# Attention's softmax on VectorE's 32x32 transposes in place of TensorE's

## The reference

```python
x = x + tanh(g_xattn) * attention(layernorm(x), ctx, ctx, mask, wq, wk, wv, wo)
#   q = rope(x @ wq), k = rope(ctx @ wk), v = ctx @ wv
#   softmax(q k^T / sqrt(128) + mask, over the 64 keys) @ v @ wo
x = x + tanh(g_ffn) * ffn(layernorm(x))
#   ((xf * in_scale) @ sign(W)^T) * out_scale + bias, scales from a softmax router
```

## Time and profile before

| | us |
|---|---|
| median of 3 runs | 1663.18 |
| span of the profiled execution (from the first to the last instruction; the page gives no other time of it) | 1658.5 |
| attention, first keys split to the last store of probabilities | 95.5 to 951.1 |
| projection, first to last w_lo | 957.0 to 1392.9 |

### The profile page before, as it was taken

How to read it: one execution, slowest core, us unless ns; L and a number is a source line. 1 busy time by engine, 2 the same in 40 slices (tenths; PEclk the granted TensorE clock), 3 DMA queues, 4 the chain that set the end, 5 groups by cost and what they waited for, 6 DMA issues and landing times. The chain is left out here.

```text
span 1658.5 us, 23370 instructions
## 1 busy us (share of the span) xinstructions
PE 1574.9 (95%) x7808; PEld 1299.9 (78%) x7808; DVE 965.7 (58%) x1670; ACT 664.2 (40%) x1271; POOL 673.3 (41%) x514
## 2 busy tenths in 40 slices
PE   6999999999999999999999689999999999389998
PEld 6878888888888888888888578888888888266776
DVE  6736666766667666666676545444444444646562
ACT  5812222322223222232222257666666665343342
POOL 6734443444434443444344234333333332323443
PEclk9999999999999999999999899999999999689999
DMA  7722212221222212222121595237923332723311
GB/s 273 255 76 64 64 45 64 70 74 39 71 63 70 63 38 71 75 64 54 52 63 38 190 366 173 77 99 269 335 77 101 101 101 78 247 76 140 119 65 58
DMA packets 90838, 183.27 MB, mean 111 GB/s; under 512 B 17152, under 2 KB 31872, under 8 KB 90752
## 3 DMA queue, kind: packets, MB, share of 16 engines
q1 hardware_dynamic: 84528, 169.94, 32.0%
q10 hardware_dynamic: 6256, 12.65, 2.1%
HBM read 129.07 MB, written 53.48 MB: 110 GB/s over the span
## 5 line engine op out<-in xcount | busy, mean ns | idle before, releaser
L46 PE MATMUL q_ps<-x_hi,w_hi 128*128 128x512 f32 x1024 | 405.1, 396 | 3.9 <-PEq L61 3.9
L48 PE MATMUL q_ps<-x_hi,w_lo 128*128 128x512 f32 x1024 | 402.2, 393 | 0.0
L47 PE MATMUL q_ps<-x_lo,w_hi 128*128 128x512 f32 x1024 | 401.3, 392 | 0.0
L869 DVE TENSOR_TENSOR vw_lo<-vw_ps,vw_hi 64x256 fp32r<-64x256 f32 x512 | 216.0, 422 | 237.5 <-ACT vw_hi L816 232.3
L594 POOL TENSOR_TENSOR q_lo<-rot,q_hi 128x512 fp32r<-128x512 f32 x128 | 191.8, 1518 | 268.4 <-ACT q_hi L563 268.4
L856 POOL TENSOR_TENSOR w_lo<-w_raw,w_hi 128x512 fp32r<-128x512 f32 x128 | 165.2, 1291 | 280.6 <-ACT w_hi L808 280.6
L816 ACT CAST vw_hi<-vw_ps 64x256 fp32r<-64x256 f32 x512 | 188.2, 368 | 142.0 <-PE vw_ps L48 130.5
L46 PEld LDWEIGHTS q_ps<-x_hi,w_hi 128*128 128x128 f32 x1024 | 192.9, 188 | 44.1 <-issue 4.1
L48 PEld LDWEIGHTS q_ps<-x_hi,w_lo 128*128 128x128 f32 x1024 | 192.6, 188 | 41.3
L47 PEld LDWEIGHTS q_ps<-x_lo,w_hi 128*128 128x128 f32 x1024 | 192.7, 188 | 40.5
L614 DVE TENSOR_TENSOR rot<-q_ps,cos_q 128x512 f32<-128x512 f32 x64 | 44.3, 692 | 288.0 <-PE q_ps L48 288.0
(11 more groups left out here) (130 smaller groups left out, 2566.4 us busy)
## 6 DMA issues: line engine op xcount, KB each, us to landing
w_raw<-in_wo SPq DMA_DIRECT2D x128, 256.0 KB, 2.6
w_raw<-in_wq SPq DMA_DIRECT2D x32, 512.0 KB, 5.2
probs_scratch<-pt_hi SPq DMA_DIRECT2D x64, 256.0 KB, 2.6
probs_scratch<-pt_lo SPq DMA_DIRECT2D x64, 256.0 KB, 3.2
x_hi<-probs_scratch SPq DMA_DIRECT2D x32, 512.0 KB, 5.9
x_lo<-probs_scratch SPq DMA_DIRECT2D x32, 512.0 KB, 7.8
x_in<-in_x SPq DMA_DIRECT2D x16, 512.0 KB, 4.1
attn_scratch<-ahead_y ACTq DMA_DIRECT2D x8, 1024.0 KB, 4.4
```

The source lines that it names most:

```text
L46: pe.matmul(out, hi, rhs_hi, start=first, stop=False, **kw)
L47: pe.matmul(out, hi, rhs_lo, start=False, stop=False, **kw)
L48: return pe.matmul(out, lo, rhs_hi, start=False, stop=last, **kw)
L869: done = nc.vector.tensor_tensor(vw_lo[at], vw_ps[i][b * SK:(b + 1) * SK, h, :], vw_hi[at].bitcast(F32), ALU.subtract)
```

## The change

The keys' heads are interleaved in blocks of 32 on the partitions of the scores: key half k, head h, 32 keys. VectorE adds the mask in the layout in which scores come (`masked`), transposes each 32x32 block of the [128, 512] tile in place of TensorE's turning, and reduces over 32 columns. A softmax row then lies in two partition halves, so the maximum and the sum are combined by a copy to PSUM and two operations of 64 partitions (`both_halves`). The product with the reciprocal is transposed again by VectorE (`pt`), ScalarE makes `pt_hi`, and GpSimd `pt_lo`, before that slot's product. The scores' copy by ScalarE and all eight turning matmuls go. The rotation keeps two products in PSUM (`rope_ps`). The stored probabilities have the interleaved order, and `load_probs` puts four blocks of 32 partitions back in the old one, one DMA each. Keys are loaded compactly and split in two halves of partitions; key_hi and key_lo are zeroed once in place of key_raw. The diff, cut:

```diff
 EARLY_P = 4
+BLK = 32
+NBLK = S // BLK
...
 def load_probs(sp, scratch, p_hi, p_lo, p_in, pair, hp):
 
     for n, part in enumerate((p_hi, p_lo)):
-        src = scratch["probs"][n, hp, :, pair * PB * S:(pair + 1) * PB * S]
-        sp.dma_start(part[:, hp].bitcast(F32), src).then_inc(p_in[hp], 16)
+        for k in range(2):
+            for h in range(2):
+                of, to = (2 * k + h) * BLK, (2 * h + k) * BLK
+                src = scratch["probs"][n, hp, of:of + BLK, pair * PB * S:(pair + 1) * PB * S]
+                sp.dma_start(part[to:to + BLK, hp].bitcast(F32), src).then_inc(p_in[hp], 16)
 
 
...
-        key_raw = sb("key_raw", [P, 2, B, P])
+        key_raw = sb("key_raw", [P, 2, B, SK])
         key_hi = sb("key_hi", [P, 2, B, P], F32R)
         key_lo = sb("key_lo", [P, 2, B, P], F32R)
         cos_q = sb("cos_q", [P, S])
         sin_q = sb("sin_q", [P, S])
-        mask = sb("mask", [P, B, TT, SK])
-        rot = sb("rot", [P, 4, S])
+        mask = sb("mask", [P, B, S])
+        prod = sb("prod", [P, 2, S])
+        rot = sb("rot", [P, 2, S])
         q_hi = sb("q_hi", [P, 2, S], F32R)
         q_lo = sb("q_lo", [P, 2, S], F32R)
-        scores_t = sb("scores_t", [P, S])
-        shifted = sb("shifted", [P, TT, 2, SK])
-        exps = sb("exps", [P, TT, 2, SK])
-        probs = sb("probs", [P, TT, 2, SK])
-        row_max = sb("row_max", [P, TT, 2])
-        row_sum = sb("row_sum", [P, TT, 2])
-        row_inv = sb("row_inv", [P, TT, 2])
+        masked = sb("masked", [P, S])
+        shifted = sb("shifted", [P, NBLK, BLK])
+        probs = sb("probs", [P, NBLK, BLK])
+        part_max = sb("part_max", [P, NBLK])
+        part_sum = sb("part_sum", [P, NBLK])
+        row_max = sb("row_max", [P, NBLK])
+        row_sum = sb("row_sum", [P, NBLK])
+        row_inv = sb("row_inv", [P, NBLK])
+        pt = sb("pt", [P, S])
         pt_hi = sb("pt_hi", [P, 2, S], F32R)
         pt_lo = sb("pt_lo", [P, 2, S], F32R)
         q_ps = [ps(f"q_ps{i}", [P, S]) for i in range(4)]
         st_ps = ps("st_ps", [P, S])
-        s_ps = ps("s_ps", [P, TT, 2, SK])
-        pt_ps = ps("pt_ps", [P, S])
+        s_ps = ps("s_ps", [P, NBLK, BLK])
+        rope_ps = ps("rope_ps", [P, S])
+        part_ps = ps("part_ps", [P, 2, NBLK])
...
         pt_lo_ready = sem("pt_lo_ready")
         pt_stored = following["pt_stored"]
 
         block = ctx.enter_context(nc.Block())
+
+        def own_block(part, h):
+
+            return part[h * HALF:(h + 1) * HALF].rearrange("f c b (k n l) -> f (c b) k n l", k=2, n=2)[:, :, :, h]
+
+        def raw_keys(h):
+
+            return key_raw[h * HALF:(h + 1) * HALF].rearrange("f c b (k l) -> f (c b) k l", k=2)
...
             def load_keys(g):
-                wait(sp, key_lo_ready, g)
+                wait(sp, key_lo_ready, 2 * g)
                 for c in range(2):
                     for h in range(2):
                         src = scratch["keys"][c].rearrange("(g f) t -> g f t", f=HALF)[bass.ds(g, 1)]
-                        sp.dma_start(key_raw[h * HALF:(h + 1) * HALF, c, :, h * SK:(h + 1) * SK],
+                        sp.dma_start(key_raw[h * HALF:(h + 1) * HALF, c],
                                      src.rearrange("o f (b s) -> (o f) b s", b=B)).then_inc(key_in, 16)
 
             def slot(g, j, last):
...
@@ -507,9 +521,9 @@
                 if has(g, j, 1):
                     b = (j - 1) % B
                     if j == 1:
-                        pe.wait_ge(key_hi_ready, g + 1)
-                        pe.wait_ge(key_lo_ready, g + 1)
-                    wait(pe, st_copied, u - 1)
+                        pe.wait_ge(key_hi_ready, 2 * (g + 1))
+                        pe.wait_ge(key_lo_ready, 2 * (g + 1))
+                    wait(pe, masked_ready, u - 1)
                     for c in range(2):
                         pe.wait_ge(q_hi_ready, 2 * u - 1 + c)
                         pe.wait_ge(q_lo_ready, 2 * u - 1 + c)
@@ -518,19 +532,6 @@
                     last.then_inc(st_done, 1)
                 if has(g, j, 0):
                     queries(g, j, 1, range(KT // 2, KT))
-                if has(g, j, 2):
-                    pe.wait_ge(probs_ready, u - 1)
-                    wait(pe, pt_hi_ready, u - 2)
-                    wait(pe, pt_lo_ready, u - 2)
-                    for i in range(TT):
-                        last = pe.transpose(pt_ps[:, i * P:(i + 1) * P], probs[:, i].rearrange("p h s -> p (h s)"), ident[:])
-                    last.then_inc(pt_done, 1)
-                if has(g, j, 1):
-                    pe.wait_ge(st_copied, u)
-                    wait(pe, masked_ready, u - 1)
-                    for i in range(TT):
-                        last = pe.transpose(s_ps[:, i].rearrange("p h s -> p (h s)"), scores_t[:, i * P:(i + 1) * P], ident[:])
-                    last.then_inc(s_done, 1)
 
...
-                    pool.wait_ge(key_hi_ready, g + 1)
-                    nc.gpsimd.tensor_tensor(key_lo[:], key_raw[:], key_hi[:].bitcast(F32), ALU.subtract).then_inc(key_lo_ready, 1)
+                    act.wait_ge(key_in, 64 * (g + 1))
+                    if isinstance(g, int) and g == 0:
+                        act.wait_ge(key_zeroed, 1)
+                    wait(act, st_done, u - 1)
+                    for h in range(2):
+                        nc.scalar.copy(own_block(key_hi, h), raw_keys(h)).then_inc(key_hi_ready, 1)
+                if has(g, j, 1):
+                    for c in range(2):
+                        act.wait_ge(rot_ready, 2 * u - 1 + c)
+                        wait(act, st_done, u - 1)
+                        nc.scalar.copy(q_hi[:, c], rot[:, c]).then_inc(q_hi_ready, 1)
+                if has(g, j, 2):
+                    act.wait_ge(shifted_ready, u - 1)
+                    nc.scalar.activation(shifted[:], shifted[:], ACT.Exp).then_inc(exps_ready, 1)
+                if has(g, j, 3):
+                    i = (j - 3) % 2
+                    act.wait_ge(pt_ready, u - 2)
+                    wait(act, pt_stored[i], 32 * (4 * g + (j - 3) // 2))
+                    nc.scalar.copy(pt_hi[:, i], pt[:]).then_inc(pt_hi_ready, 1)
+                if j % B == B - 1 and not (last and j >= B):
+                    split_w(hp + 1, 0)
+
+            over_key_heads(act, slot, True)
+
+        @block.gpsimd
+        def _(pool):
+            def split_w(hp, c):
+                pool.wait_ge(w_hi_ready, 2 * (hp - 1) + c + 1)
+                nc.gpsimd.tensor_tensor(w_lo[:, c], w_raw[:, c], w_hi[:, c].bitcast(F32), ALU.subtract).then_inc(w_lo_ready, 1)
+
+            def slot(g, j, last):
+                u = STEPS_G * g + j
+                hp = 2 * g + j // B
+                if j % B == 0 and has(g, j, 0) and not (isinstance(g, int) and g == 0 and j == 0):
+                    split_w(hp, 1)
+                if j == 1:
+                    for h in range(2):
+                        pool.wait_ge(key_hi_ready, 2 * g + h + 1)
+                        nc.gpsimd.tensor_tensor(own_block(key_lo, h), raw_keys(h), own_block(key_hi, h).bitcast(F32),
+                                                ALU.subtract).then_inc(key_lo_ready, 1)
+                        pool.wait_ge(key_lo_ready, 2 * g + h + 1)
                 if has(g, j, 1):
                     for c in range(2):
                         pool.wait_ge(q_hi_ready, 2 * u - 1 + c)
-                        nc.gpsimd.tensor_tensor(q_lo[:, c], rot[:, 2 * c], q_hi[:, c].bitcast(F32),
+                        nc.gpsimd.tensor_tensor(q_lo[:, c], rot[:, c], q_hi[:, c].bitcast(F32),
                                                 ALU.subtract).then_inc(q_lo_ready, 1)
+                if has(g, j, 3):
+                    i = (j - 3) % 2
+                    pool.wait_ge(pt_hi_ready, u - 2)
+                    wait(pool, pt_stored[i], 32 * (4 * g + (j - 3) // 2))
+                    nc.gpsimd.tensor_tensor(pt_lo[:, i], pt[:], pt_hi[:, i].bitcast(F32), ALU.subtract).then_inc(pt_lo_ready, 1)
                 if has(g, j, 2):
                     pool.wait_ge(inv_ready, u - 1)
-                    wait(pool, pt_done, u - 2)
-                    nc.gpsimd.tensor_tensor(probs[:], exps[:], row_inv[:].unsqueeze(3).to_broadcast([P, TT, 2, SK]),
+                    wait(pool, pt_ready, u - 2)
+                    nc.gpsimd.tensor_tensor(probs[:], shifted[:], row_inv[:].unsqueeze(2).to_broadcast([P, NBLK, BLK]),
                                             ALU.mult).then_inc(probs_ready, 1)
                 if j % B == B - 1 and not (last and j >= B):
                     split_w(hp + 1, 0)
@@ -605,43 +612,65 @@
 
         @block.vector
         def _(dve):
+            def both_halves(out, part, moved, op):
+
+                for half in range(2):
+                    here, there = (slice(n * SK, (n + 1) * SK) for n in (half, 1 - half))
+                    done = nc.vector.tensor_tensor(out[here], part[here], moved[there], op)
+                return done
+
             def slot(g, j, last):
```

(84 more changed lines are left out.)

6 lines of the change are left out of this document (removed).

## The result

The changed kernel takes 1674.37 us (median of 4 runs, 1669.62 to 1675.84) against 1661.72 us of the kernel before on the same chip: ratio 1.0062, interval 1.0046 to 1.0079. It is slower by 0.6%, where a faster one was forecast (1641). Attention did become shorter; the projection took more than that back.

A forecast was written before the change was run, and what follows sets the result against it. TensorE, busy 95%, was taken to bound the kernel. -55.6 + 22 + 2.5 + 9 = -22 us gave a span of 1636.5, a median of 1641; the forecast's own range was 1628 to 1656, the whole range 1618 to 1690.

The forecast's parts named there:

- Loading probabilities: Projection: 8 loads of 32 partitions per head pair in place of 2 of 128 make weights land late, +9 us.
- issue term for the first quarter: Projection's first quarter: SP's 9.7 issues of 0.45 us take 4.35 per head pair against TensorE's 3.43; weights land 1011.3, needed 1003.
- in the later replacement ... nothing: Later reload of probabilities, 16 head pairs: SP needs 4.05 us against 3.5, a 9 us lag, costing nothing.
- lead of four buffers: Later reload of probabilities: the four buffers run some 11 us ahead, enough to cover SP's 9 us lag.
- half-rate rival: Projection loads and attention's end: 32-partition loads write SBUF slower, near 200 GB/s; +21 us in all, 1685; chance 0.24.
- break-even of 230 GB/s: Projection loads: below about this rate the slower narrow loads outweigh the change's gain.
- Removed from TensorE: Attention steps: without the turning matmuls TensorE saves 0.89 us per step, 62.5 times, -55.6 us.
- VectorE's chain: Attention step: VectorE's work with transposes at 0.69 us takes 9.7 of 12.36 us, so it fits.
- Subtractions without stretching: Attention, VectorE: subtracting the maximum, with one input from PSUM, takes 0.68 us and no longer stretches beside GpSimd.
- GpSimd's chain: Attention, each new head pair: the weights' low part queues behind new GpSimd work; TensorE loses 1.5 us, 15 times, +22 us.
- End of the stage: Attention's last steps, with no queries to hide under: from last rotation to last store 20.2 us against 18.1, +2.5 us.
- The stall costs clock: Attention: 1.5 us of idle TensorE lowers its clock, 15 times some 2 us more, 1671; chance 0.05.

The follow-up runs named there:

- e3: Changed kernel with each head pair's probabilities loaded by 8 DMAs over all 128 partitions, a quarter of the columns each, reordering left out: 1659.8 us, ratio 0.9973.
- e11: Changed kernel with whole loads (2 DMAs of 128 partitions, reordering left out) plus six DMAs of 256 bytes per head pair: 1657.66 us, ratio 0.996.
- e5: Changed kernel with 4 loads of 64 partitions per head pair in place of 8 of 32, reordering left out: 1687.39 us, ratio 1.0165.
- e9: Changed kernel with the same 8 loads of 32 partitions, issued to targets 0, 32, 64, 96 in place of 0, 64, 32, 96: 1689.76 us, ratio 1.0176.
- e6: Changed kernel with the first half of the next head pair's weights split earlier in the step, on ScalarE and GpSimd: 1644.92 us, ratio 0.9912.
- e1: Changed kernel with whole loads of probabilities, 2 DMAs of 128 partitions per head pair, reordering left out: 1632.47 us, ratio 0.981.
- e8: Changed kernel with the low part of the probabilities moved from GpSimd to VectorE, behind the reciprocal: 1668.49 us, ratio 1.0049.

## Why the prediction was wrong

The failing step is **Loading probabilities**, +9 forecast and +31.5 measured.
- It priced narrow loads by SP's issues alone and took the full rate for granted; the rows bore only on 128 partitions. The rate in the changed kernel is 265 to 282 GB/s at a full DMA share, where the kernel before has 383 and 400, and below the 310 that SP's issues alone would allow (8 x 128 KB + 256 KB + 128 KB in 10 x 0.465 = 4.65 us; e3 and e11 show 301 and 306). So the rate sets the pace, not the issues. As an estimate, 1.44 MB at 278 GB/s take 5.2 us a head pair, 0.5 more than the issues, which is 6 us for 12 of them; the first quarter lost 16.3 against e11's 10.8.
- Its issue term for the first quarter was nearly right in size: 0.465 us an issue where 0.45 was assumed, ten issues where it counted 9.7, +10.8 in e11 against +9 (its own numbers, 1011.3 against 1003, give 8.3).
- Its "in the later replacement ... nothing" was wrong: e11 shows +6.8 and +1.2 there. Nine issues take 4.19 us against 3.5, a lag of 11 us over 16 head pairs, of which 8 were lost. The lead of four buffers that I let absorb 9 us absorbed about 3.
- The half-rate rival (0.24) named the place, the mechanism and the sign. With the narrow loads at some 250 GB/s (an estimate, below) its own sum gives 956.5 + 12 x 4.96 + 4 - 1003 = +17 in the first quarter, which fits the 16.3, but only 16 x 1.15 - 11 - 5 = +2 in the replacement, where 15.2 were lost. So it too counted on leads that are not there, and its break-even of 230 GB/s was too low.

The Trainium skill ("SBUF — State Buffer", Door 1: The DMA port swizzle) says that 64 partitions move no faster than 32. The runs agree: e5 and e9 lose the same, at 234 to 257 and 235 to 251 GB/s. Its 189 GB/s is of one transfer of 1 MiB over 32 partitions, and its limit for such a span is about 218. The windows count all that DMA moves, and 0.375 of each 1.375 MiB here went over 128 partitions; if these moved at 390 GB/s, the narrow loads alone ran at some 215 in e9 (an estimate from its 245), close to that limit, and at some 250 in the changed kernel (from its 278). So the order of targets 0, 64, 32, 96 gained about 15%. The Trainium skill (the same page, "Can I just issue two DMAs to hit both halves?") has 6% for two DMAs at partitions 0 and 64; here, with many in flight, the measurement decides.

The other steps:
- *Removed from TensorE,* -55.6: e6, without the stall, has 63 steps of 12.32, 776.1, against 833.1: -57.0. Right.
- *VectorE's chain,* transposes at 0.69: 0.727 into PSUM and 0.70 into SBUF. The estimate of 0.71 from the Trainium skill ("VectorE: DVE Perf Modes", The three transpose paths) was as good. Subtractions without stretching: 0.69 in all 64. Right.
- *GpSimd's chain,* +22: steps of 13.8 to 14.2 us stand 15 times among those of 12.3; e6 gives 26.9. Right in mechanism, 0.3 us each too low: dependent rotation operations through PSUM are spaced 0.82, not 0.72, and TensorE starts 0.25 after w_lo's end, not 0.09.
- *End of the stage,* +2.5: +4.7; e1 shows 1.5 of it without the early narrow loads.
- *The stall costs clock:* 1.00 from 104 to 900 us. Rightly rejected. Where TensorE waited longer, in the projection, the clock did fall (0.74 over 1180 to 1200, with 10.6 of 20 us busy); what that cost apart from the waiting is not shown.

By the measured terms: -57 + 27 + 4.7 + 31.5 = +6, and 3 ahead of attention, inside the scatter of its start.

## What to carry to other kernels

A reordering by DMA has its price where the queue is full: here eight narrow DMAs a head pair cost 35 us as loads in a saturated stretch (31.5, and 3.2 at the stage's end), and eight a step under 6 as stores in one that used a quarter of it. (Stores also go the other way, out of SBUF; no run has narrow stores in a full stretch, so direction and fullness are not told apart.) Price a split transfer twice, by issues times their spacing and by bytes over the rate of its partition span, compare the larger with the consumer's rhythm, and do not add them. When work moves to an engine with slack, look at what is queued behind it in the one step where that matters; a change of order took back 27 us that the move had cost.

## What the runs showed of the hardware

- The order of narrow loads matters: targets 0, 64, 32, 96 gave 265 to 282 GB/s (all traffic of the core), targets 0, 32, 64, 96 235 to 251 (e9), with the DMA share near 1.05 in both; whole loads 383 to 404, at 1.02 to 1.04. A full share says nothing of the bytes.
- Slow rate and many issues do not add: 49.8 us lost with four narrow loads a head pair (e5), 49.1 with eight (e9), 18.8 by eight issues alone (e11).
- SP issues a DMA each 0.465 us whether it moves 128 KB or 256 bytes; six that move next to nothing, a head pair, added 18.8 us to a projection of 436.
- A VectorE transpose of 32x32 float32 blocks in 128x512 takes 0.727 us into PSUM and 0.701 into SBUF.
- GpSimd's product beside VectorE's subtraction with two SBUF inputs: 1.38 us in place of 1.05 (e8).
